# Where a graph attention's running totals are kept: SBUF with VectorE, or one PSUM bank with ScalarE

## The reference

```python
h = (x @ W.T).reshape(n, H, D)                      # H = 8 heads, D = 32
alpha = einsum('ehd,hd->eh', h[src], a_src) + einsum('ehd,hd->eh', h[dst], a_dst)
enc = relu(edge_attr @ edge_W.T + edge_b).reshape(-1, H, D)
alpha = leaky(alpha + sum(enc * h[dst], axis=-1))
ex = exp(alpha - segment_max(alpha, dst)[dst])
denom = segment_sum(ex, dst)
out = segment_sum(h[src] * (ex / max(denom[dst], 1e-10))[..., None], dst)
```

## Time and profile before

| | |
|---|---|
| runs | 2431.32, 2416.58, 2420.48 us |
| median of the 3 runs | 2420.48 us |
| profiled execution, its span from first to last instruction | 2421.0 us (no other time is given for it) |
| the attention stage in it | from its first instructions near 1408 us to 2074.7 us |
| granted TensorE clock, mean of the execution | 0.881 of full speed |

### The profile page before, as it was taken

One profiled execution on the slowest core, in us unless ns is written; L12 is line 12 of the kernel. 1 busy time (PEld: TensorE's weight loads), 2 busy tenths in 40 slices (PEclk: granted clock), 3 DMA queues, 4 the chain that ended last, 5 costly groups with the idle time before them and its releaser, 6 DMA issues. The chain is left out here.

```text
span 2421.0 us, 41392 instructions
## 1 busy us (share of the span) xinstructions
PE 1785.6 (74%) x11452; PEld 1386.4 (57%) x11452; DVE 1638.0 (68%) x3379; ACT 805.9 (33%) x2077; POOL 1152.8 (48%) x1106
## 2 busy tenths in 40 slices
PE   3466666655179996399992878888887887499598
PEld 1245445544057775299991546666665665255587
DVE  8655565555167778655556849999999999764443
ACT  7433333322000002333331644444444444244221
POOL 0277777777700000055550057777777776000243
PEclk9677887887589999599996889999999999799799
DMA  3355555544388862522225145555555553533353
GB/s 86 110 190 192 188 189 173 172 167 165 128 298 284 294 216 103 200 64 73 71 68 180 39 146 146 145 150 142 151 152 145 145 144 113 194 131 119 123 180 104
DMA packets 203758, 368.03 MB, mean 152 GB/s; under 512 B 63193, under 2 KB 111162, under 8 KB 203159
## 3 DMA queue, kind: packets, MB, share of 16 engines
q1 hardware_dynamic: 148066, 205.99, 26.2%
q0 software_dynamic: 54624, 159.35, 21.3%
q10 hardware_dynamic: 850, 0.04, 0.0%
HBM read 235.32 MB, written 130.87 MB: 151 GB/s over the span
## 5 line engine op out<-in xcount | busy, mean ns | idle before, releaser
L2136 POOL DMA_INDIRECT att_rows<-hdram,top_ix x440 | 502.8, 1143 | 264.0 <-issue 133.8
L874 POOL DMA_INDIRECT mtab<-first_w,msgs_ix x280 | 277.5, 991 | 85.3 <-issue 81.1
L1177 POOL IOTA route_spare<- 128x65 f32 (+1 forms) x2 | 0.4, 177 | 522.3 <-POOLq L1115 522.3
L2217 PE MATMUL att_p_acc<-att_msg,att_hot 128*128 128x264 f32 x880 | 225.8, 401 | 14.7 <-DVE wts_wn L2396 6.5
L736 PE MATMUL msgs_p_m<-nodes_n,msgs_hott 128*128 x592 | 185.1, 467 | 48.8 <-issue 30.7
L2251 ACT ACTIVATE att_enc<-att_p_z 128x1024 f32<-128x1024 f32 x110 | 112.7, 1024 | 308.8 <-PE att_p_z L2157 308.8
L2217 PEld LDWEIGHTS att_p_acc<-att_msg,att_hot 128*128 128x128 f32 x880 | 163.4, 196 | 53.2 <-issue 26.6
L874 POOL DMA_INDIRECT mtab<-msgs_rw,msgs_ix x160 | 160.6, 1004 | 68.9 <-issue 44.8
L2166 PE MATMUL att_p_h<-heads_parts,att_hz 128*128 x1320 | 184.3, 295 | 1.4 <-DVE att_enc L2323 1.4
L637 DVE TENSOR_TENSOR first_w<-msgs_p_m,msgs_sorted 128x1024 f32<-128x1024 f32 x70 | 85.6, 1223 | 140.3 <-PE msgs_p_m L736 113.1
L736 PEld LDWEIGHTS msgs_p_m<-nodes_n,msgs_hott 128*128 128x128 f32 x592 | 132.4, 235 | 76.7 <-issue 56.0
(11 more groups left out here) (408 smaller groups left out, 3811.7 us busy)
## 6 DMA issues: line engine op xcount, KB each, us to landing
first_w<-mtab SPq DMA_DIRECT2D x77, 520.0 KB, 4.6
etab<-msgs_et SPq DMA_DIRECT2D x110, 288.0 KB, 2.5
att_hz<-etab SPq DMA_DIRECT2D x110, 288.0 KB, 2.9
msgs_rw<-mtab SPq DMA_DIRECT2D x45, 520.0 KB, 4.7
htab<-hid_hr SPq DMA_DIRECT2D x12, 1024.0 KB, 4.3
first_w<-in_L_ffn_w SPq DMA_DIRECT2D x16, 512.0 KB, 5.0
ffn0x_w<-in_L_ffn_w SPq DMA_DIRECT2D x16, 512.0 KB
ffn_w<-in_L_ffn_Wd SPq DMA_DIRECT2D x8, 1024.0 KB
```

The costliest lines, as they stand in the source:

```text
L874: nc.gpsimd.indirect_dma_start(mtab, bass.IndirectOffsetOnAxis(ap=ix[:, g, q:q + 1], axis=0), rw[g % RS][:, q, :], None).then_inc(s_free[g ...
L2136: nc.gpsimd.indirect_dma_start(rows[:, g % RS, q, :], None, hdram, bass.IndirectOffsetOnAxis(ap=ix1[:, g, q:q + 1], axis=0)).then_inc(s_ro ...
L2217: last = T.matmul(p_acc[u % 2][:, 0:HW], hot[g % 2][:, q, :], msg[g % 2][:, q, :], start=(r == 0), stop=(r == UQ - 1))
```

## The change

Now there is one bank, `p_sum`, and it is never cleared after the first unit: the matmuls of every unit add to what stands in it (`start` is set for unit 0 alone). ScalarE copies the bank to `acc` after each unit and then multiplies the bank in place by the keep flags of the next unit, a factor for each partition. Where a new block begins, VectorE (`lessen`) multiplies it by `fall`. VectorE's additions, the four total tiles and two of the semaphores go. The sums of a group's two units stand apart: the first at the head of TensorE's step, the second between `encoders` and `destinations`. ScalarE's copies stand in the same way before and after `encodings`. The loop has LAG + 1 more steps than groups, where it had LAG + 3.

```diff
-            def sums(g):
-                pe.wait_ge(s_msg, g + 1)
-                pe.wait_ge(s_wide, g + 1)
-                pe.wait_ge(s_weight, g + 1)
-                for u in range(g * GU, (g + 1) * GU):
-                    if u >= 2:
-                        pe.wait_ge(s_add, u - 1)
-                    for r in range(UQ):
-                        q = u % GU * UQ + r
-                        last = T.matmul(p_acc[u % 2][:, 0:HW], hot[g % 2][:, q, :], msg[g % 2][:, q, :],
-                                        start=(r == 0), stop=(r == UQ - 1))
-                    last.then_inc(s_acc, 1)
+            def sums(u):
+                g, t = u // GU, u // BU
+                if u % GU == 0:
+                    pe.wait_ge(s_msg, g + 1)
+                    pe.wait_ge(s_wide, g + 1)
+                    pe.wait_ge(s_weight, g + 1)
+                if u % BU:
+                    pe.wait_ge(s_same, u - t)
+                elif t:
+                    pe.wait_ge(s_less, t)
+                for r in range(UQ):
+                    q = u % GU * UQ + r
+                    last = T.matmul(p_sum, hot[g % 2][:, q, :], msg[g % 2][:, q, :], start=(u == 0 and r == 0),
+                                    stop=(u == NU - 1 and r == UQ - 1), skip_group_check=True)
+                last.then_inc(s_acc, 1)
...
-            for s in range(NUG + LAG + 3):
-                t, j = s // BG, s % BG
+            for s in range(NUG + LAG + 1):
+                t, j, at = s // BG, s % BG, (s - LAG - 1) * GU
+                if 0 <= at < NU:
+                    sums(at)
...
+                if 0 <= at < NU:
+                    sums(at + 1)
+                if s + 1 < NUG:
                     destinations(s + 1)
...
-                if 0 <= s - LAG - 1 < NUG:
-                    sums(s - LAG - 1)
...
+            def keep_totals(u):
+                b = act.value_load(gb[0:1, u:u + 1], min_val=0, max_val=NT - 1)
+                act.wait_ge(s_acc, u + 1)
+                if u:
+                    act.wait_ge(s_kept, u)
+                S.copy(acc[:, bass.ds(b, 1), :].rearrange("p a c -> p (a c)"), p_sum).then_inc(s_kept, 1)
+                if (u + 1) % BU and u + 1 < NU:
+                    act.wait_ge(s_kept, u + 1)
+                    S.mul(p_sum, p_sum, keep[:, u + 1:u + 2]).then_inc(s_same, 1)
...
-                if 0 <= s - LAG - 3 < NUG:
-                    keep_totals(s - LAG - 3)
+                if 0 <= at < NU:
+                    keep_totals(at)
                 if s + 1 < NUG:
                     encodings(s + 1)
+                if 0 <= at < NU:
+                    keep_totals(at + 1)
...
+            def lessen(t):
+                dve.wait_ge(s_fall, t + 1)
+                dve.wait_ge(s_kept, t * BU)
+                V.tensor_tensor(p_sum.rearrange("p (h d) -> p h d", d=D + 1), p_sum.rearrange("p (h d) -> p h d", d=D + 1),
+                                bc(fall[t % 2][:], 2, D + 1), ALU.mult).then_inc(s_less, 1)
...
+                if 0 < at < NUG and at % BG == 0:
+                    lessen(at // BG)
...
-                if 0 <= s - LAG - 2 < NUG:
-                    for u in range((s - LAG - 2) * GU, (s - LAG - 1) * GU):
-                        gathered(u)
```

More of the change, by code:

```diff
@@ L2064, in split, with attention @@
     link(V.tensor_copy(parts[2], rest))
-def attention(nc, a, cst, etab, segtab, ewz, ix1, penn, gb, keep, hparts, hdram, acc, spare):
-    RS, SE, TS = 12, 10, 4
+def attention(nc, a, cst, etab, segtab, ewz, ix1, penn, gb, keep, hparts, hdram, acc):
+    RS, SE = 12, 10
     two = range(2)
@@ L2089, in attention @@
     fall = [a.sb(f"fall{s}", [P, H]) for s in two]
-    total = [a.sb(f"total{s}", [P, HW])[:] for s in two] + [lent[:, 0:HW] for lent in spare]
     ex = [a.sb(f"ex{s}", [P, BC, H]) for s in two]
@@ L2094, in attention @@
     p_z = a.ps("p_z", [P, G, C])
-    p_acc = [a.ps(f"p_acc{s}", [P, 512]) for s in two]
+    p_sum = a.ps("p_sum", [P, 512])[:, 0:HW]
     p_adst = a.ps("p_adst", [P, 512])
@@ L2099, in attention @@
     (s_z, s_enc, s_h, s_prod, s_red, s_adst, s_al, s_line, s_chain, s_rb, s_back, s_backc, s_top, s_new, s_fall, s_edge,
-     s_dif, s_ex, s_msg, s_wide, s_acc, s_add, s_go, s_weight, s_kept) = (a.sem(m) for m in (
+     s_dif, s_ex, s_msg, s_wide, s_acc, s_same, s_less, s_weight, s_kept) = (a.sem(m) for m in (
          "z", "enc", "h", "prod", "red", "adst", "al", "line", "chain", "rb", "back", "backc", "top", "new", "fall", "edge",
-         "dif", "ex", "msg", "wide", "acc", "add", "go", "weight", "kept"))
+         "dif", "ex", "msg", "wide", "acc", "same", "less", "weight", "kept"))
     s_rows, s_hz, s_seg = ([a.sem(f"{m}{s}") for s in range(k)] for m, k in (("rows", RS), ("hz", SE), ("seg", 2)))
@@ L2275, in falls @@
                 S.activation(fall[t % 2][:], fall[t % 2][:], ACT.Exp).then_inc(s_fall, 1)
-            def keep_totals(g):
-                for u in range(g * GU, (g + 1) * GU):
-                    b = act.value_load(gb[0:1, u:u + 1], min_val=0, max_val=NT - 1)
-                    act.wait_ge(s_add, u + 1)
-                    if u:
-                        act.wait_ge(s_kept, u)
-                    S.copy(acc[:, bass.ds(b, 1), :].rearrange("p a c -> p (a c)"), total[u % TS][:]).then_inc(s_kept, 1)
+            def keep_totals(u):
[7 more added lines that the diff above has]
+                    S.mul(p_sum, p_sum, keep[:, u + 1:u + 2]).then_inc(s_same, 1)
             def exponents(t):
@@ L2402, in _ @@
             link(V.memset(turns[:], -2.0 * BIG))
-            link(V.memset(total[TS - 1][:], 0.0))
-            for s in range(NUG + LAG + 3):
-                t, j = s // BG, s % BG
+            for s in range(NUG + LAG + 1):
+                t, j, at = s // BG, s % BG, s - LAG - 1
+                if 0 < at < NUG and at % BG == 0:
+                    lessen(at // BG)
                 if s < NUG:
@@ L2486, in build @@
                 with ExitStack() as c1:
-                    attention(nc, Pool_(nc, c1, "att"), cst, etab, segtab, ewz, ix1, penn, gb[1], buckets[1], hparts, hdram, acc,
-                              [wts["wn"][:].rearrange("p k c -> p (k c)"), wts["gabe"][:].rearrange("p r c -> p (r c)")])
+                    attention(nc, Pool_(nc, c1, "att"), cst, etab, segtab, ewz, ix1, penn, gb[1], buckets[1], hparts, hdram, acc)
             reuse_semaphores(nc)
```

16 lines of the change are left out of this document (removed).

## The result

The changed kernel takes 2462.66 us (median of 4 runs, 2459.56 to 2464.69), the kernel before 2422.57 in runs beside it: a ratio of 1.0158, interval 1.0139 to 1.0177. That is slower by 1.4 to 1.8%; the forecast was 2456 us in a range of 2430 to 2490. The profiled execution of the changed kernel spans 2457.8 us, against 2421.0 before: +36.8 us.

A forecast was written before the change was run, and what follows sets the result against it. GpSimd and VectorE run full side by side before; TensorE and ScalarE together bound the changed kernel. Steady part 20, head 2 and drain 16 give +38, taken as +35 on 2421: 2456 us, range 2430 to 2490.

The forecast's parts named there:

- the new ring: Attention stage: one bank makes each unit a strict round of TensorE matmuls, ScalarE copy and multiplication; block 23.7 us against 23.34.
- The block, forecast +0.81: Steady part, four groups: 0.36 us longer by the steps plus 0.45 for the clock, over 25 blocks +20 us.
- step-by-step sum of 23.7: A block's four steps from first sums to next first sums, read at full clock: 5.7 + 5.0 + 6.3 + 6.7 us.
- the second step: Step of a block where tops stands before the offsets: 6.7 us, of which 3.3 from first sums to encoders.
- The clock term: Steady part: some 9 us of TensorE execution per block at a mean clock of 0.95 cost 0.45 us more.
- The drain, forecast +16: Last eight groups after the last gather: 5.0 us a group without a second bank, 39 us against 23.3.
- rival C: TensorE idles twice a step, its mean clock falls to 0.85: +70, 2491 us; chance 0.15 together with rival D.
- The head, forecast +2: Stage's head and first two blocks: the new ring counts only from the eighth step on, +2 us.
- The multiplication: ScalarE's added in-place 128x264 multiplication by a per-partition factor in PSUM: taken as 0.49 us, bounds 0.41 and 0.60.
- Rival D: In-place PSUM multiplication much dearer than 0.6 us, or engines disturb each other; at 1.0 us 2490; chance 0.15 with rival C.
- GpSimd cannot by more than the collisions: Attention stage: GpSimd's gathers, full today, can speed up only by their collisions with message multiplications: 20.1 against 23.3 us a block.
- rival A: VectorE's relief counts: block 22.3 us, near GpSimd's limit, time falls by 9 to 2412 us; chance 0.12.

The follow-up runs named there:

- e1_widen_early: Changed kernel with weights and widen moved ahead of the encodings and the second copy on ScalarE: 2388.8 us, 0.9851 of the kernel before.
- e10_early_twice: Changed kernel with weights and widen early and ScalarE's keep-flag multiplication done twice per unit: 2460.5 us, 1.0143 of the kernel before.
- e6: Changed kernel with four idle TensorE matmuls after each unit's sums, in the drain alone: 2448.0 us, 1.0093 of the kernel before.
- e7: Changed kernel with both early weights and widen and the drain's idle matmuls: 2371.4 us, 0.9777 of the kernel before.

## Why the prediction was right

**The sign and the mechanism.** The ring of TensorE and ScalarE replaced GpSimd and VectorE as the bound, in the words of the prediction's part on the new ring, and the waits after are those it named. The whole came out at +40 us between medians, +36.8 between profiles, forecast +35. But the terms erred, in opposite directions: the drain was forecast 14 us too short, the steady part 7 and the head 2 too long, 3 had been taken off the sum for a better overlap, and 6.4 fell away in parts of the program that the change leaves alone. That the total met within 2 us is luck.

**The block, forecast +0.81, measured +0.54.** At full clock the step-by-step sum of 23.7 was too long. Two neighbouring blocks of the changed kernel, the first at full clock:

```profile
1663.51:1686.49 22.98, 17.73 (x171) 13.97 (x170) 18.36 (x26) 13.21 (x31) 15.26 (x16) 1.00 0.52 148
1686.49:1710.77 24.28, 19.18 (x171) 14.66 (x171) 18.29 (x26) 13.23 (x31) 16.28 (x17) 0.93 0.50 145
```

22.98 is 0.36 under the kernel before, not over it. The full-clock block's steps, from first sums to first sums as in the forecast, last 6.23, 6.24, 5.64 and 4.91 us, forecast 6.3, 6.7, 5.7 and 5.0. So most of the excess of 0.7 is one term, the second step, and in it the 3.3 us from the first sums to the encoders:

```profile
1671.36 1.13 PE L2219 MATMUL att_p_sum<-att_msg,att_hot 128*128 128x264 f32 x4 [1.04 <-ACT att_hot L2271]
...
1674.28 0.59 PE L2156 MATMUL att_p_z<-top_ewz,att_hz 128*128 128x512 bf16 x2 [1.11 <-issue]
...
1677.60 1.13 PE L2219 MATMUL att_p_sum<-att_msg,att_hot 128*128 128x264 f32 x4
```

They are 1674.28 - 1671.36 = 2.92.

The clock term was too small: a mean of 0.94 cost 23.88 - 22.98 = 0.90 a block and not 0.45. The forecast spread the loss evenly over the 9 us of TensorE on the ring. In the trace it comes in whole stretches at the lower level, 56 of 61 us of them in a block's second step, the one with `tops` (in 1694 to 1701 us the clock is 0.76 and the step takes 7.6 us, not 6.24). That the steady part also held such a mean before, at no cost, the prediction had seen, and it is so: the blocks of before with 3.4 us at the lower level last 23.10 in the mean, those with none 23.45. The ring took away the cover.

**The drain, forecast +16, measured +31.** Those are the eight groups, 54.3 - 23.3; from the last full block's row it is +29.7. The term was sized at full clock, as the drain before ran: 5.0 us a group, 39 for eight. Measured are 7.15 and 54.3, at a clock of 0.50. That the clock would stay up with TensorE waiting in every round was the step without support, and the drain's clock was the missing mechanism; with the clock near the top (0.93) the eight groups take 41.4, close to the 39. The prediction had put its worry on the clock into the steady part (rival C) and not into the drain, where TensorE has nothing but the ring's two bursts. The Trainium skill (TensorE: Matmul & The Clock Gate, "A second HAM failure mode: psum-queue depth-cycling") tells of a kernel whose clock swings between the two levels because TensorE idles briefly, again and again, between groups of matmuls as PSUM banks come round. The steady part's swings, 0.94 in the mean, are of that kind; the drain does not swing, it stays at 0.50 to its end.

**The head, forecast +2, measured 0.**

**The multiplication.** In 1480 to 2040 us, by groups:

```profile
L2290 ACT ACTIVATE att_p_sum<-att_p_sum,plan_bucket 128x264 f32<-128x264 f32 x164 | 74.7, 455 | 5.4
L2287 ACT COPY sum_acc<-att_p_sum 128x264 f32 x187 | 70.9, 379 | 145.8 <-PE att_p_sum L2219 145.4
```

0.455 us, inside 0.41 to 0.60 and 0.03 under the estimate, and the copy takes 0.379 from PSUM where it took 0.412 from SBUF. Rival D is out. In the forecast's own sum stand three copies and two multiplications a block, so these two prices are 0.17 of the 0.7 by which it was too long. The claim of the Trainium skill that the prediction cites (ScalarE: Activation LUTs, "Step-by-step: what each stage is for"), that ScalarE writes faster to PSUM, would have given 0.41; no run multiplied into both memories, so the traces neither bear it out nor refute it.

**"GpSimd cannot by more than the collisions", and the floor.** The remark that "the gathers get almost nothing from the change" was wrong: 1.15 fell to 1.01 us a gather. It cost the forecast nothing, since GpSimd was waiting anyway. But rival A was weighed with it: its "22.3, near GpSimd's limit" was no limit: e1_widen_early runs at 20.95, and removing the additions alone gives 21.59. (16 x 1.25 is 20.0, not 20.1; nothing hangs on it.) The relief of VectorE is worth 44 us; the ring ate all of it and 13 more. What the prediction had right is the reason: "ScalarE's order is fixed and widen comes last". With widen moved, and with nothing else, rival A's time of 2412 is beaten by 23 us.

What freed the gathers can be read from where they start. In 1480 to 2040 us of the kernel before, 91 of 383 start in the first microsecond of a message multiplication and lose 76 us by it; in the changed kernel it is 39 of 382, and 21 us. Those 55 us are nearly all of the 57 by which GpSimd's busy time fell. The removed operations themselves slowed hardly anything. Of the 42 gathers that start inside L2396 or L2393 none took over 0.97 us:

```profile
1557.67 0.49 DVE L2396 SCALAR_TENSOR_TENSOR att_total<-att_total,plan_bucket,att_p_acc 128x264 f32<-128x264 f32 x1
...
1557.94 0.95 POOL L2136 DMA_INDIRECT att_rows<-hdram,top_ix  x1 [0.30 <-issue]
```

The 12 that start inside L2390 took 0.99 to 1.06. This agrees with the rule that the prediction cites from the Trainium skill (SBUF — State Buffer, "SBUF: two separate sides"), which counts only operations with two SBUF inputs, and those only against a GpSimd operation that reads SBUF; a gather reads its row numbers there. So the rule was right about the removed operations. The prediction's step from it was not: the same collisions with the same multiplication became fewer, because the gathers started elsewhere. Some of them had no choice: the 48 that waited for VectorE's messages were released when a multiplication ended.

## What to carry to other kernels

When work moves from a full engine to an idle one, its cost is not the new engine's busy time, but the place at which it stands in that engine's order: what the other engines need next must come first in the queue (here one move of widen turned +1.6% into -1.5%). A single accumulator makes a serial round of two engines; price it with the clock that TensorE gets when it works in short bursts, above all where it has no other work, as in a drain. And before a limit is called a floor, ask whether it holds apart from the collisions: 23.3 us of gathers were 20.95.

## What the hardware showed unexpectedly

What slows a gather is almost only a start inside VectorE's message multiplication, and early enough in it. In the kernel before the 91 gathers that start in its first microsecond take 1.06 to 1.95 us; the 289 that start outside it take at most 1.08. In e1_widen_early (timeline, GpSimd and VectorE):

```profile
1704.37 0.96 POOL L2135 DMA_INDIRECT att_rows<-hdram,top_ix  x1 [0.30 <-issue]
...
1704.45 1.22 DVE L2388 TENSOR_TENSOR att_msg<-att_rows,att_ex 128x1024 f32<-128x1024 f32 x1
...
1710.08 1.22 DVE L2388 TENSOR_TENSOR att_msg<-att_rows,att_ex 128x1024 f32<-128x1024 f32 x1
...
1710.69 1.44 POOL L2135 DMA_INDIRECT att_rows<-hdram,top_ix  x1 [0.30 <-issue]
```

The first started 0.08 us ahead of the multiplication and took 0.96; the other started inside one, and ended at 1710.69 + 1.44 = 1712.13, 0.83 after its end at 1711.30, as in the earlier trace rows. So what the same gather costs depends on the phase of the two engines' loops: 1.15 us in the mean before, 1.00 in e1_widen_early. Why one version keeps the better phase is not shown. By the rule of the Trainium skill (SBUF — State Buffer, "SBUF: two separate sides") whichever of the two starts first holds the port pair for its whole instruction, and the other is blocked. For the gathers both rows come out so. For the multiplication they do not: the one that began inside a gather took the usual 1.22 us, and the 24 of the kernel before that began inside one took 1.22 to 1.24. Of the 0.83 us behind the operation's end the rule says nothing.

The clock can settle into either of two patterns in one program: e10_early_twice ran blocks of 22.3 us at 1.00 and then, from about 1550 us on, blocks of 23.9 at 0.93 to the end. And 16 times four idle matmuls in the drain made the program 14.7 to 17.4 us shorter (e6 against the changed kernel, e7 against e1).
